# Softmax division of P inside the group's own step, weight maxima at the end of the step, and another set of groups that are divided before P V

## The reference

```python
q = layernorm(x) @ w_q.T                       # 32 heads of 32
k, v = ctx @ w_k.T, ctx @ w_v.T                # 8 groups of 32, 4 heads each
scores = where(mask, q k^T / sqrt(32), min)    # per head 128 x 128
out = softmax(scores) @ v
x = x + out @ w_out.T
x1, x2 = split(layernorm(x) @ w12.T + b12)
return x + (silu(x1) * x2) @ w3.T + b3
```

## Time and profile before

| | us |
|---|---|
| median of 3 runs (lowest to highest) | 1055.39 (1055.15 to 1059.57) |
| the profiled execution | 1057.56 |
| its span, first to last instruction | 1055.7 |
| PE busy | 1017.3 (96% of the span) |
| DVE busy | 694.5 (66%) |
| POOL busy | 528.2 (50%) |
| ACT busy | 476.3 (45%) |

### The profile page before, as it was taken

The page is one execution under the profiler, slowest core; times in us unless marked ns, Lnnn a source line. Parts: engine busy times, 40 slices in busy tenths (PEclk is TensorE's granted clock), DMA queues, the critical chain, the costliest instruction groups (busy, mean ns, idle before and its releaser), DMA issues.

```text
span 1055.7 us, 22106 instructions
## 1 busy us (share of the span) xinstructions
PE 1017.3 (96%) x8320; PEld 678.1 (64%) x8320; DVE 694.5 (66%) x2160; ACT 476.3 (45%) x1303; POOL 528.2 (50%) x501
## 2 busy tenths in 40 slices
PE   8898899998989989999999999999999999999998
PEld 7787757767667666686655544444444888468853
DVE  6889987878788778887747422836865446625431
ACT  6768566666566666665675420123431111211110
POOL 2779923835537447378977698138752301213000
PEclk9999999999999989999999999999999999999999
DMA  9669676897988968989974725295759641874201
GB/s 364 232 169 186 157 197 169 195 260 208 230 211 210 222 189 238 224 211 234 250 188 101 214 106 200 67 323 188 265 186 207 240 121 41 210 248 121 81 31 50
DMA packets 230779, 199.13 MB, mean 189 GB/s; under 512 B 177040, under 2 KB 187280, under 8 KB 225808
## 3 DMA queue, kind: packets, MB, share of 16 engines
q1 hardware_dynamic: 230672, 197.72, 68.4%
HBM read 119.04 MB, written 35.65 MB: 147 GB/s over the span
## 4 chain that ended last, share of the span: by engine, by line
PE 60%; DVE 5%; DMA 4%; SPq 1%; ACT 1%; POOL 1%; issue 1%; DVEq 0%
PE bank_dense L1407 37%; PE bank_spare L1407 6%; PE bank_score L1563 6%; PE bank_spare L1563 5%; DMA arena_rows<-w_t 3%; PE bank_av L1563 3%; DVE arena_in L1727 2%; DVE arena_attn L1891 1%; PE bank_score L1464 1%; POOL arena_attn L975 1%; SPq L738 1%; DMA arena_rows<-x_scratch 1%; ACT arena_attn L1203 0%; PE bank_spare L1416 0%; ACT arena_attn L1218 0%
## 5 line engine op out<-in xcount | busy, mean ns | idle before, releaser
L1407 PE MATMUL bank_dense<-arena_rows,arena_in 128*128 128x256 f16 (+1 forms) x1272 | 176.9, 296 | 1.8 <-POOL arena_in L913 0.9
L975 POOL TENSOR_TENSOR arena_attn<-arena_attn 128x512 f16<-128x512 f32 x89 | 103.9, 1185 | 125.6 <-ACT arena_attn L1218 125.6
L1407 PE MATMUL bank_dense<-arena_attn,arena_rows 128*128 128x512 f16 x768 | 166.4, 379 | 0.0
L1407 PEld LDWEIGHTS bank_dense<-arena_rows,arena_in 128*128 128x128 f16 x1272 | 122.6, 98 | 45.0 <-DVE arena_in L1739 1.3
L1891 DVE CUSTOM_DVE_ANT_0 arena_attn<-bank_score,arena_in 128x128 f32<-128x128 f32 x512 | 143.6, 345 | 1.2 <-PE bank_score L1464 0.9
L1407 PEld LDWEIGHTS bank_dense<-arena_attn,arena_rows 128*128 128x128 f16 x768 | 75.2, 98 | 90.2
L1407 PE MATMUL bank_dense<-arena_out,arena_attn 128*128 128x512 f16 x576 | 127.8, 379 | 1.0 <-DVE arena_attn L1931 0.5
L1203 ACT ACTIVATE arena_attn<-arena_attn,arena_in 128x128 f32<-128x128 f32 x320 | 124.0, 391 | 6.0 <-DVE arena_in L1891 4.9
L1218 ACT ACTIVATE arena_attn<-arena_attn 128x1024 f16<-128x1024 f32 x64 | 67.5, 1055 | 97.9 <-DVE arena_attn L1913 97.6
L1407 PEld LDWEIGHTS bank_dense<-arena_out,arena_attn 128*128 128x128 f16 x576 | 55.4, 98 | 64.7 <-DVE arena_attn L1931 0.7
L1407 PE MATMUL bank_spare<-arena_rows,arena_in 128*128 128x256 f16 (+1 forms) x648 | 87.7, 292 | 0.0
(11 more groups left out here) (237 smaller groups left out, 1898.3 us busy)
## 6 DMA issues: line engine op xcount, KB each, us to landing
arena_rows<-x SPq DMA_DIRECT2D x32, 512.0 KB, 6.0
arena_in<-w_scratch SPq DMA_DIRECT2D x64, 256.0 KB, 3.0
arena_attn<-q_scratch SPq DMA_DIRECT2D x48, 256.0 KB, 4.3
arena_rows<-w_t SPq DMA_DIRECT2D x12, 1024.0 KB, 6.7
arena_rows<-ctx_t SPq DMA_DIRECT2D x8, 1024.0 KB, 5.8
q_scratch<-arena_attn SPq DMA_DIRECT2D x16, 512.0 KB, 5.3
x_scratch<-arena_rows SPq DMA_DIRECT2D x16, 512.0 KB, 3.9
arena_out<-x_scratch SPq DMA_DIRECT2D x16, 512.0 KB, 6.0
```

The source lines that it names most:

```text
L975: ins = pool.tensor_tensor(p_split[:, g % 2, u, 1], e[:, g % 2, u], p_split[:, g % 2, u, 0], ALU.subtract)
L1407: ins = pe.matmul(dst, lhs(a, c), rhs(b, c), start=(c == chunks[0] and n == 0), stop=(c == chunks[-1] and n == 2))
```

## The change

The set `NORMED` was 8 to 47 and is now 12 to 47 and 56 to 63. For 56 to 63 VectorE divides both halves. In VectorE's list, `norm_prob(g, 1)` moves from the start of step g + 1 into step g, ahead of the second unit's low part (in t = 8's feed-forward steps right behind half 0); `norm_prob(g, 0)` moves ahead of the first unit's low part; the weight maximum moves behind the second unit's low part. TensorE's three tail steps call `weigh` for groups 61 to 63 instead of `turn_attn`.

```diff
-NORMED = range(8, 48)
+NORMED = [*range(12, 48), *range(56, 64)]
...
 def by_pool(g):
-    return g in NORMED and g % GROUPS >= 3
+    return g in NORMED and g % GROUPS >= 3 and g < 56
...
             for s in (8, 9, 10):
                 hidden(0, H_AT[s], 0)
-                turn_attn(NG - 11 + s)
-                if s < 10:
-                    weigh(NG + s - 10)
+                weigh(NG - 11 + s)
                 hidden(0, H_AT[s], 1)
...
             def norm_prob(g, u):
-                sums_inv = (inv_first if g < NORMED[2] else inv_bank)[:, g % 2, u]
+                sums_inv = (inv_first if g - 2 not in NORMED else inv_bank)[:, g % 2, u]
...
-                    if g - 1 in NORMED:
-                        norm_prob(g - 1, 1)
                     if g >= 3:
                         divide(g - 3)
                     mask_scores(g)
...
                         prob_lo(g - 1)
+                    if g in NORMED:
+                        norm_prob(g, 0)
+                    if g in NORMED and t == NB and s in H_AT:
+                        norm_prob(g, 1)
                     unit_lo(first_unit(t, s))
...
                         attn_lo(g - 3)
-                    if g in NORMED:
-                        norm_prob(g, 0)
                     if t < NB - 1 and s == 5:
                         max_of(f"ctx{t + 1}", ctx_next, s_ctxload, 16 * t + 32)
-                    if look_at(t, s):
-                        max_of(look_at(t, s), look, s_look, look_count(look_at(t, s)))
-                    if look_at(t, s) == "w7":
-                        in_pairs()
...
+                    if g in NORMED and not (t == NB and s in H_AT):
+                        norm_prob(g, 1)
                     if tile2 is not None:
                         x_lo(tile2, 0)
                         x_lo(tile2, 1)
                     unit_lo(second_unit(t, s))
+                    if look_at(t, s):
+                        max_of(look_at(t, s), look, s_look, look_count(look_at(t, s)))
+                    if look_at(t, s) == "w7":
+                        in_pairs()
```

## The result

| | us |
|---|---|
| before, median of 4 runs (lowest to highest) | 1057.48 (1055.15 to 1061.23) |
| changed, median of 4 runs | 1043.64 (1040.64 to 1045.69) |
| ratio, 95% interval | 0.9864 (0.9821 to 0.9906) |
| predicted | 1039.5 (1035.5 to 1048) |
| profiled execution of the changed kernel, its span | 1045.69, 1043.9 |

The changed kernel is 1.4% faster. The forecast was a gain of 16.0 us. Between the medians it is 13.8, between the two profiled executions 11.9.

What follows compares the result with a forecast made beforehand. PE, busy 1017.3 of 1055.7 us, was taken as the bound, with DVE pacing block 2. Gains 4.2 + 9.8 - 0.6 + 0.5 + 2.1 = 16.0 us gave 1039.5 us, range 1035.5 to 1048.

Steps and rivals of the forecast that it cites:

- Part A: Block 2: groups 8 to 11 not divided before P V; gain 4.2 us, from 2.0 to 4.7.
- Part B: Step 7 of blocks 3, 4, 5: earlier mask and load, clock staying up; gain 9.8 us, 5.0 of it clock.
- The mask: Step 7 of block 3: mask of group 23 starts 3.17 us behind PE's scores in place of 4.53.
- the rest: Step 7: PE's work left behind its second wait, 3.64 us at full clock.
- the term of 0.3 for half 0's factor: Step 7: 0.3 us added before PE's second wait ends, half 0's reciprocal and factor now preceding v's low part.
- Part C: Step 7 of block 6: maximum and two pairing instructions now follow the low part; loss about 0.6 us (0 to 1.5).
- 7.73: Step 7 of block 6: us into the step at which PE's second wait ends, formerly 7.19.
- Part D: Block 7: PE's one wait for an output's low part goes; gain 0.5 us (0 to 0.5).
- Part E: Groups 56 to 63 divided before P V: PE has 0.26 us less in each of eight steps; gain 2.1 (0 to 2.1).
- Rival 1: Steps 7 of blocks 3 to 6: remaining idle still lowers the clock; gain 9.8, 1045.6 us; chance 0.20.
- Rival 2: Step 7: the maximum stays in the mask's way, its load not issued sooner; gain 6.8, 1048.6 us; chance 0.12.
- Rival 3: Blocks 3 to 6: slower, as DVE waits twice for ACT in its own step; about 1066 us; chance 0.06.

Runs made afterwards that it cites:

- head_only: Kernel before, with only groups 8 to 11 no longer divided before P V; order and tail as before: 1054.0 us, ratio 0.9964.
- norm_only: Kernel before, with only the two halves of the division moved into the group's own step, the weight maximum staying ahead: 1047.04 us, ratio 0.99.
- max_only: Kernel before, with only the weight maximum moved behind the second unit's low part: 1056.65 us, ratio 0.9989.
- max6_back: Changed kernel, with step 6's maximum and the pairing instructions back at their old place ahead of half 1: 1036.13 us, ratio to before 0.9793.
- pairs_later: Changed kernel, with the two small pairing instructions moved behind the mask of group 47: 1040.4 us, ratio to before 0.9833.
- no_tail: Changed kernel without groups 56 to 63 in the divided set: 1045.35 us, ratio to before 0.9881.
- order_only: Changed kernel's VectorE order, with the old set of groups 8 to 47 and the old tail: 1051.7 us, ratio to before 0.9941.
- max_in7_a: Changed kernel, with step 6's maximum and the pairs moved into step 7, ahead of the second unit's low part: 1046.9 us.

## Why the prediction was right, and where not

- Direction and size held: 1043.64 lies in the range, 4.1 above the forecast, 2.1 of which is the median of before. In the profiles the five parts add up to 15.1 against 16.0, but that closeness is in part luck: B came out 1.6 and D 0.6 better than forecast, C 2.2 and E 0.9 worse.
- Part A came to 4.27 for 4.2, and head_only shows it to be the set's. Two of its terms missed by half a microsecond each and cancelled. TensorE's idle time in block 2 fell by 4.7 us in place of 5.2 (5.20 to 0.49), since the wait for v's low part in step 7 stayed at 0.4; and its busy time grew by 0.4 in place of 1.0.
- Part B was 1.6 us too small. The mask (3.16 for 3.17) and the rest (3.64) were exact, the term of 0.3 for half 0's factor was wrong by itself. But the reason given for the gain was half right. The prediction had both the earlier load and the maximum's new place; norm_only and max_only show that the move of the division carries most of it (8.6 of the 11.4 us in blocks 3 to 5), and that the maximum's move brings nothing alone. With the load early the new place makes the steps alike, but max6_back, with the old one, is faster. "The load is issued at 225 to 226" was right (225.77), by the wrong releaser: the context's maximum holds it, in the kernel before half of the time already, and the prediction names P alone.
- Part C is the step that failed: "a loss of about 0.6 (0 to 1.5)" was 3.0 in step 7 of block 6 (2.8 for the block). Its 7.73 is 3.17 + 0.33 + 3.93 + 0.3, with the pairs at the 0.33 us that they took in the kernel before; they took 1.73 beside GpSimd, the waits grew to 3.5 us, and the clock fell for 1.4 more. pairs_later gives the 3 us back. "Here no load was late" was also too much: block 6 lies behind a weight maximum too, and VectorE waited 0.91 us for its load, which had landed by the scores:

```profile
440.41 2.29 DVE L1727 TENSOR_REDUCE arena_in<-arena_rows 128x1 f32<-128x2048 f32 x1 [0.91 <-DMA arena_rows<-w_t]
```

- Part D was 1.1 for 0.5. Step 3 of block 7, where the wait was, gave 0.7, and norm_only has that as well; the rest is step 7 of block 7, 9.12 for 9.53. That step took 9.12 in max_only and 9.1 to 9.7 in the others, so it isn't the division's.
- Part E was 1.2 for 2.1. TensorE's shorter steps came (6.18 for 6.45 us), but step 3 of block 8 gained a wait of 0.71 for the output's low part (0.7 to 1.2 in the other profiles with this tail). ScalarE takes P's high part, a table load (1.28 us), an activation and the high part of that output in this order, in no_tail too. What is new is that P's high part now waits 1.51 us for VectorE's division (L1911), and all behind it with it. no_tail shows the net, 1.3.
- Rival 1 is a matter of size and chance. The clock stayed up in blocks 3 to 5 of the changed kernel in both profiles, and fell in block 3 of order_only and of no_tail with the same waits. Rival 2's ground fell: the maximum had no wait. Rival 3 didn't come, since the 0.63 and 1.11 us waits of VectorE in its own step lay in its spare time; with 2.3 us more in max_in7_a they no longer did. Where between them that turns, no run shows.

## What to carry to other kernels

When an instruction waits for a load, follow the load's issue back to all that it waits for, counts of semaphores included: here an elementwise division moved, and a transpose in SyncE's queue and an unrelated maximum on VectorE, which both held the load, came sooner; moving the waiting instruction alone did nothing. When small instructions are moved, look at what GpSimd does at the new place, not at their old duration. And here a late operation did best where its engine idled anyway, with its data safely there, rather than at the end of the step or past the next critical one.

## What the runs showed of the hardware

- VectorE's 128x4 TENSOR_TENSOR and COPY within SBUF took 0.62 to 0.64 and 1.03 to 1.09 us beside a subtraction of GpSimd and 0.14 to 0.17 alone.
- TensorE's granted clock fell to its lower level, 1.2 GHz, in every profiled step 7 whose waits came to 2.7 us or more, and in none whose one wait was 0.45 to 0.63. Where it fell, the rest behind the last wait was 4.8 to 5.3 us in place of 3.6, and 6.0 to 6.5 in the three steps in which it stayed low longer (block 5 of before, blocks 3 and 4 of head_only). Between the two it did both. With 1.07 + 0.62 it stayed up in 13 of 15 steps (all six of the two profiles of the changed kernel) and fell in block 3 of order_only and of no_tail, and with 1.01 + 0.67 it fell in block 4 of max6_back; with 0.80 + 0.67, 1.34 + 0.66, 1.19 + 0.71 and 1.07 + 0.89 it stayed up. The Trainium skill, "TensorE: Matmul & The Clock Gate", section "What's actually happening", says of the start of a kernel that the same program stays throttled for a different time in each run. The traces show the like for gaps in its middle, in that the same two waits, 1.07 and 0.62, end both ways; no run tells what decides it.
- The same 1 MB load for step 6 took 5.6 to 8.5 us from issue to landing in different blocks and kernels. Within max6_back it was 6.0 us in block 3 and 7.5 in block 4, and the steps 7 took 9.34 and 12.16, 2.8 us apart.
